# Second layer of a two-layer state-space network: the decay factors move from PSUM to SBUF, and the freed PSUM banks go to other matmul outputs

## What is computed

```
xc = silu(conv2d(x_in));  xz = in_proj(xc);  xm, z = split(xz)
xm = silu(causal_conv1d(xm) + bias)                 # 3 taps, per channel
dt_r, Bm, Cm = split(x_proj(xm));  dt = softplus(dt_proj(dt_r) + dt_b)
for every token t:                                  # 96 channels, 16 states each
    h = exp(dt * A) * h + (dt * xm) * B             # A per channel and state
    y = sum over states of h * C
out = out_proj((y + D * xm) * silu(z)) * silu(x_gate)
```

## Time and profile before

| | |
|---|---|
| median of 3 runs | 1569.81 us (1568.59 to 1570.61) |
| the profiled execution's own time | 1570.93 us |
| its span | 1569.0 us |
| `mid1_phase` in it | from about 676 us to about 1422 us |
| busy shares of the whole span | DVE 77%, PE 74%, ACT 71%, POOL 60% |

### The profile page before, as it was taken

How to read it: one execution, slowest core, us unless ns; L and a number is a source line. 1 busy time by engine, 2 the same in 40 slices (tenths; PEclk the granted TensorE clock), 3 DMA queues, 4 the chain that set the end, 5 groups by cost and what they waited for, 6 DMA issues and landing times. The chain is left out here.

```text
span 1569.0 us, 14783 instructions
## 1 busy us (share of the span) xinstructions
PE 1155.8 (74%) x3828; PEld 423.9 (27%) x3828; DVE 1205.6 (77%) x1198; ACT 1107.2 (71%) x1643; POOL 947.1 (60%) x501
## 2 busy tenths in 40 slices
PE   4899636665643777777888888888888888455995
PEld 2343101111102555422222222222222222002663
DVE  1666539998982777604999999999999999992775
ACT  2687257767642777648889889888888888741664
POOL 2500059999993333216988988888888889850000
PEclk8999855555556999978888888888888888666997
DMA  5455450301002233218878777788777886616572
GB/s 144 123 145 141 98 173 17 108 0 41 14 28 86 84 94 100 76 45 213 191 181 190 183 173 171 178 187 185 177 171 180 183 186 158 155 44 131 127 176 56
DMA packets 137487, 200.56 MB, mean 128 GB/s; under 512 B 27099, under 2 KB 69130, under 8 KB 136916
## 3 DMA queue, kind: packets, MB, share of 16 engines
q1 hardware_dynamic: 133964, 193.27, 50.1%
q0 software_dynamic: 1280, 3.74, 0.8%
q10 hardware_dynamic: 2160, 2.61, 0.7%
HBM read 145.93 MB, written 53.63 MB: 127 GB/s over the span
## 5 line engine op out<-in xcount | busy, mean ns | idle before, releaser
L1802 DVE TENSOR_TENSOR_SCAN m_h<-m_qa,m_state,m_ub 128x512 f32<-128x512 f32 x384 | 464.1, 1263 | 63.7 <-POOL m_ub L1389 56.9
L1389 POOL TENSOR_TENSOR m_ub<-m_dlb,m_bt 128x1536 f32<-128x1536 f32 x128 | 440.4, 3441 | 16.5 <-DMA m_dlb<-scratch_dldu 6.0
L1753 ACT ACTIVATE m_qa<-m_dlb,k_a 128x512 f32<-128x512 f32 x384 | 250.9, 681 | 56.7 <-DVE m_h L1802 52.1
L1813 DVE TENSOR_TENSOR m_g<-m_h,m_qc 128x1536 f32<-128x1536 f32 x128 | 221.4, 1730 | 10.0 <-DVE m_h L1802 8.6
L1596 PE MATMUL m_qm<-m_xa,k_u_taps 96*96 96x512 f32 x192 | 152.3, 959 | 32.3 <-ACT m_sz L1681 31.6
L1635 PE MATMUL m_qy<-m_g,k_seld 128*32 128x512 f32 x768 | 157.9, 697 | 0.0
L1110 POOL TENSOR_TENSOR b_u<-b_dl,b_z 128x1024 f32<-128x1024 f32 x48 | 130.3, 2714 | 17.9 <-ACT b_dl L1000 16.1
L1121 POOL TENSOR_TENSOR b_y<-b_y,b_g 128x1024 f32<-128x1024 f32 x48 | 135.9, 2830 | 3.4 <-DVE b_g L1073 3.2
L1618 PE MATMUL m_qc<-m_cp,k_selc 112*128 112x512 bf16 x128 | 52.3, 409 | 105.7 <-DVE m_g L1813 105.7
L966 PE MATMUL b_qb<-b_bc,k_pack_sel 96*128 96x512 bf16 x96 | 58.9, 613 | 94.8 <-DVE b_u L1051 94.7
L1411 POOL TENSOR_TENSOR m_rest<-m_bcr,m_cp 16x512 f32<-16x512 f32 x32 | 36.9, 1152 | 105.3 <-ACT m_cp L1722 76.1
(11 more groups left out here) (191 smaller groups left out, 2350.5 us busy)
## 6 DMA issues: line engine op xcount, KB each, us to landing
m_dlb<-scratch_dldu SPq DMA_DIRECT2D x128, 384.0 KB, 9.9
m_bt<-scratch_brow SPq DMA_DIRECT2D x128, 256.0 KB, 5.8
scratch_dldu<-m_dldu SPq DMA_DIRECT2D x32, 384.0 KB, 3.2
scratch_z<-a_z SPq DMA_DIRECT2D x24, 256.0 KB
scratch_y<-b_y SPq DMA_DIRECT2D x12, 512.0 KB, 2.6
c_y<-scratch_y SPq DMA_DIRECT2D x16, 384.0 KB, 3.4
scratch_gate<-m_gt SPq DMA_DIRECT2D x32, 192.0 KB, 3.7
scratch_y<-m_yo SPq DMA_DIRECT2D x32, 192.0 KB, 11.5
```

The source lines that it names most:

```text
L1389: nc.gpsimd.tensor_tensor(ub[k % 3][:], dlb[u % 2][:, J:2 * J, :], bcast(bt[u % 2][:, n, :], J), ALU.mult).then_inc(ub_ready, 1)
L1753: nc.scalar.activation(q_a[:, j, :], dlb[u % 2][:, j, :], ACT.Exp, scale=G["a1"][:, j, n:n + 1]).then_inc(da, 1)
L1802: nc.vector.tensor_tensor_scan(h[k % 3][:, j, :], q_a[:, j, :], ub[k % 3][:, j, :], state[:, k % NS, j:j + 1], ALU.mult, ALU.add).then_inc ...
L1813: nc.vector.tensor_tensor(g[k % 2][:], h[k % 3][:], bcast(q_c[:], J), ALU.mult).then_inc(read, 1)
```

## The change

The decay moves to two SBUF buffers, `m_qa0` and `m_qa1`; a decay of step k+1 now waits for the scan of step k-1, not of step k. The three freed banks go out as follows: `m_qm` is split into `m_qu` (causal products) and `m_qz` (z), `m_qg` into `m_qg` (gate) and `m_qt` (dt, B and C rows), and `m_qy` gets a second buffer. With a bank of its own the causal product is no longer evicted to `m_acc`; the SiLU reads `m_qu`. On ACT the softplus of unit t+2 stands in `window` behind the SiLUs, with one table load fewer in each unit, `y_evict` goes to s = 3 and `keep` one step later. On POOL `du_of` goes behind the drive of its step and `outputs` behind `least_of`. On SP the store of y goes to s = 0, ahead of the store of B rows. On PE the projections are dealt out to other steps.

```diff
-        q_a = m.ps("m_qa", [P, J, CH])
-        q_c = m.ps("m_qc", [P, CH])
-        q_y, q_f, q_m = (m.ps(f"m_q{n}", [DI, CH]) for n in ("y", "f", "m"))
-        q_g = m.ps("m_qg", [P, CH])
+        qa = [m.sb(f"m_qa{r}", [P, J, CH]) for r in range(2)]
+        q_y = [m.ps(f"m_qy{r}", [DI, CH]) for r in range(2)]
+        q_f, q_u, q_z, q_g = (m.ps(f"m_q{n}", [DI, CH]) for n in ("f", "u", "z", "g"))
+        q_t, q_c = (m.ps(f"m_q{n}", [P, CH]) for n in ("t", "c"))
...
             def decay(k):
...
-                    if k >= 1:
-                        act.wait_ge(scanned, 3 * (k - 1) + j + 1)
-                    nc.scalar.activation(q_a[:, j, :], dlb[u % 2][:, j, :], ACT.Exp,
+                    if k >= 2:
+                        act.wait_ge(scanned, 3 * (k - 2) + j + 1)
+                    nc.scalar.activation(qa[k % 2][:, j, :], dlb[u % 2][:, j, :], ACT.Exp,
                                          scale=G["a1"][:, j, n:n + 1]).then_inc(da, 1)
...
-                    nc.vector.tensor_tensor_scan(h[k % 3][:, j, :], q_a[:, j, :], ub[k % 3][:, j, :],
+                    nc.vector.tensor_tensor_scan(h[k % 3][:, j, :], qa[k % 2][:, j, :], ub[k % 3][:, j, :],
                                                  state[:, k % NS, j:j + 1], ALU.mult, ALU.add).then_inc(scanned, 1)
...
             def dt_of(v):
...
-                pe.wait_ge(gt_ready, min(v + 2, UNITS))
-                nc.tensor.matmul(q_g[:], G["wdt"][:], xm[v % 4][:], start=True, stop=True).then_inc(dt_mm, 1)
+                if v >= 1:
+                    pe.wait_ge(delta, v)
+                    pe.wait_ge(bc_out, v)
+                    pe.wait_ge(top_out, v)
+                nc.tensor.matmul(q_t[:], G["wdt"][:], xm[v % 4][:], start=True, stop=True).then_inc(dt_mm, 1)
...
-                act.wait_ge(u_mm, v + 1)
-
-                if v >= 1:
-                    act.wait_ge(xm_ready, v)
-                nc.scalar.activation(acc[:], q_m[:], ACT.Identity).then_inc(u_out, 1)
...
             def step(t, s, k):          # GpSimd
+                drive(k + 2)
                 if s == 2:
                     du_of(t + 2)
-                drive(k + 2)
-                if s == 2:
-                    outputs(t - 1)
...
                 if s == 3:
-                    alone(k + 3, t + 3, t)
+                    alone(k + 3, t + 3, t - 1)
                     least_of(t + 2)
+                    outputs(t - 1)
...
             def step(t, s, k):          # ScalarE
                 decay(k + 1)
-                keep(k)
+                keep(k - 1)
+                if s == 0:
+                    rows_out(t + 2)
                 if s == 1:
-                    y_evict(t - 1)
-                    window(t + 4, t + 3)
+                    window(t + 4, t + 3, t + 2)
                 if s == 2:
                     tail_of(t + 5)
-                    u_of(t + 4)
                     middle(t + 2)
                 if s == 3:
-                    softplus(t + 3)
-                if s == 0:
-                    rows_out(t + 2)
+                    y_evict(t - 1)
```

More of the change, by code:

```diff
@@ L1567, in gate_of @@
                     pe.wait_ge(gt_ready, v)
[L1568 to L1572, removed]
+                nc.tensor.matmul(q_g[:], G["gate64"][64:64 + C, :], cva[v % 2][64:64 + C, 0:CH], start=True,
                                  stop=True).then_inc(gate_mm, 1)
@@ L1578, in z_of @@
                 pe.wait_ge(xa_ready, v + 1)
-                pe.wait_ge(u_out, v + 1)
-                nc.tensor.matmul(q_m[:], G["l1_min_z"][:], xa[v % HIST][:, 2:2 + CH], start=True, stop=True).then_inc(z_mm, 1)
+                if v >= 1:
+                    pe.wait_ge(sz_ready, v)
+                nc.tensor.matmul(q_z[:], G["l1_min_z"][:], xa[v % HIST][:, 2:2 + CH], start=True, stop=True).then_inc(z_mm, 1)
             def u_of(v):
@@ L1593, in u_of @@
                 if v >= 1:
-                    pe.wait_ge(sz_ready, v)
+                    pe.wait_ge(xm_ready, v)
                 for k in range(3):
-                    last = nc.tensor.matmul(q_m[:], G["u_taps"][:, k, :], xa[v % HIST][:, k:k + CH], start=(k == 0),
+                    last = nc.tensor.matmul(q_u[:], G["u_taps"][:, k, :], xa[v % HIST][:, k:k + CH], start=(k == 0),
                                             stop=(k == 2))
@@ L1623, in skip_of @@
                 pe.wait_ge(xm_ready, v + 1)
-                nc.tensor.matmul(q_y[:], G["dmat"][:], xm[v % 4][0:DI, :], start=False, stop=False).then_inc(skip_mm, 1)
+                nc.tensor.matmul(q_y[v % 2][:], G["dmat"][:], xm[v % 4][0:DI, :], start=False, stop=False).then_inc(skip_mm, 1)
             def add_up(k):
@@ L1630, in add_up @@
                 pe.wait_ge(read, k + 1)
-                if n == 0 and u >= 1:
-                    pe.wait_ge(y_out, u)
+                if n == 0 and u >= 2:
+                    pe.wait_ge(y_out, u - 1)
                 for j in range(J):
-                    last = nc.tensor.matmul(q_y[32 * j:32 * j + 32, :], G["seld"][:], g[k % 2][:, j, :],
+                    last = nc.tensor.matmul(q_y[u % 2][32 * j:32 * j + 32, :], G["seld"][:], g[k % 2][:, j, :],
                                             start=(n == 0), stop=(n == 3))
@@ L1640, in step @@
                 if s == 0:
+                    skip_of(t - 1)
+                    conv_low(t + 4)
+                if s == 1:
                     z_of(t + 3)
[L1642 to L1644 removed]
                     gate_of(t + 4)
                 if s == 2:
[L1647 removed]
+                    conv_pairs(t + 5)
                     dt_of(t + 3)
                 if s == 3:
[L1650 removed]
+                    u_of(t + 4)
                 c_of(k)
@@ L1657, in _, with window @@
         def _(act):
[L1659 to L1662, removed]
+            def window(a, b, c):
+                if exists(a) or exists(b):
+                    act.preload_act_table_set(SILU_SET)
                 if exists(a):
@@ L1680, in window @@
                         act.wait_ge(y_ready, b - 4)
-                    nc.scalar.activation(sz[b % 5][:], q_m[:], ACT.Silu).then_inc(sz_ready, 1)
-                    act.wait_ge(u_out, b + 1)
+                    nc.scalar.activation(sz[b % 5][:], q_z[:], ACT.Silu).then_inc(sz_ready, 1)
+                    act.wait_ge(u_mm, b + 1)
                     if b >= 4:
@@ L1686, in window @@
                         act.wait_ge(du_ready, b - 3)
-                    nc.scalar.activation(xm[b % 4][0:DI, :], acc[:], ACT.Silu, bias=G["l1_c1b"][:, 0:1]).then_inc(xm_ready, 1)
-                act.preload_act_table_set(LOG_EXP_SET)
+                    nc.scalar.activation(xm[b % 4][0:DI, :], q_u[:], ACT.Silu, bias=G["l1_c1b"][:, 0:1]).then_inc(xm_ready, 1)
+                if exists(a):
+                    act.wait_ge(gate_mm, a + 1)
+                    if a >= 2:
+                        act.wait_ge(gt_stored[a % 2], 16 * (a // 2))
+                    nc.scalar.activation(gt[a % 2][:], q_g[:], ACT.Silu).then_inc(gt_ready, 1)
+                softplus(c)
+                if exists(a) or exists(b) or exists(c):
+                    act.preload_act_table_set(LOG_EXP_SET)
             def tail_of(v):
@@ L1717, in rows_out @@
                     act.wait_ge(brow_stored[v % 4], 16 * (v // 4))
-                nc.scalar.activation(bcr[v % 4][DI:P, :], q_g[DI:P, :], ACT.Identity).then_inc(bc_out, 1)
+                nc.scalar.activation(bcr[v % 4][DI:P, :], q_t[DI:P, :], ACT.Identity).then_inc(bc_out, 1)
                 if v >= 4:
                     act.wait_ge(c_mm, 4 * (v - 4) + 4)
-                nc.scalar.activation(cp[v % 4][DI:DI + NS, :], q_g[DI:DI + NS, :], ACT.Identity).then_inc(top_out, 1)
+                nc.scalar.activation(cp[v % 4][DI:DI + NS, :], q_t[DI:DI + NS, :], ACT.Identity).then_inc(top_out, 1)
             def middle(v):
@@ L1739, in softplus @@
                     act.wait_ge(dldu_stored[v % 2], 16 * (v // 2))
-                nc.scalar.activation(dldu[v % 2][:, 0, :], q_g[0:DI, :], ACT.Softplus).then_inc(delta, 1)
-                act.preload_act_table_set(LOG_EXP_SET)
+                nc.scalar.activation(dldu[v % 2][:, 0, :], q_t[0:DI, :], ACT.Softplus).then_inc(delta, 1)
             def decay(k):
@@ L1762, in y_evict @@
                     act.wait_ge(y_ready, v)
-                nc.scalar.activation(yq[:], q_y[:], ACT.Identity).then_inc(y_out, 1)
+                nc.scalar.activation(yq[:], q_y[v % 2][:], ACT.Identity).then_inc(y_out, 1)
             def keep(k):
```

17 lines of the change are left out of this document (5 added, 12 removed).

## The result

| kernel | median us | ratio to before, 95% interval |
|---|---|---|
| before (same chip) | 1570.21 | |
| changed | 1890.48 (1886.38 to 1893.24) | 1.2031 [1.1995, 1.2067] |

The change costs 320 us; forecast were 1905 us and a range of 1830 to 1995. The profiled execution took 1893.24 us, its span is 1891.4 us.

A forecast was written before the change was run, and what follows sets the result against it. DVE was taken to bound the loop at 5.19 us a step; with scans and POOL's drives excluding each other, 8.04. The loop's +335 us and -1 for the rest on 1570.9 gave 1905 us, range 1830 to 1995.

The forecast's parts named there:

- The bound: Loop of the kernel before: DVE bounds it at 5.19 us a step; at most 24 us of waits can be won.
- The conflict carried over from L1286 to the scan: Scans with two SBUF inputs and POOL's drives exclude each other, as product L1286 and POOL do; chance 0.85.
- The step: Loop: the first scan is blocked until the drive ends; 7.01 us without small products, 8.04 with them, now 5.19.
- The small products: Four POOL products a unit, 1.21 us a step, each slipping between two scans: +1.03 us a step.
- The loop: First scan to last product: 125 steps of 8.04 us, three of 5.19, some 3 us at the end: 1023, +335.
- Start-up: The stretch from 676 to 728 us, before the first scan: a change of 0, +-8 us.
- The PSUM read: Scans lose a PSUM read: 3.5 us less at most, taken as 0; the skill's fixed costs would give 25.
- ACT's Exp into SBUF: On ACT: 681 ns could become 600 or 800, 0.36 us a step, hidden.
- the first rival: Scans take no part in the conflict: DVE stays at 5.19 us a step, 1547 to 1572 us; chance 0.06.
- `window` in one piece: On ACT: four SiLUs, three loads and the softplus, about 6.8 us; fits in 8.04, would overrun at 5.19.
- The third rival: Scans and drives exclude each other and POOL misses DVE's product: 9.7 us a step, 2113 us; chance 0.04.
- the second rival: Scans and drives take turns by element: POOL bounds the loop at 6.2 us a step, 1677 us; chance 0.05.

The follow-up runs named there:

- e6: e2 with `du_of` again ahead of the drive of its step on POOL; result not the reference's: 1543.46 us, ratio 0.9829.
- e1: The kernel before with only the decay moved, to one SBUF buffer in place of the three PSUM banks: 1926.27 us, ratio 1.2257.
- e2: The changed kernel with the scan's second input a PSUM bank of zeros, y eviction at s = 1; result not the reference's: 1602.41 us, ratio 1.0215.
- e3: The changed kernel with each drive made for only the first half of a unit's tokens; result not the reference's: 1692.03 us in one run.
- e4: The changed kernel with each drive replaced by two memsets of zero, which only write SBUF; result not the reference's: 1592.71 us in one run.
- e9: The changed kernel with `du_of` again ahead of the drive of its step on POOL: 1927.88 us, ratio 1.2262.
- e5: The kernel before, decay in PSUM, with `c_of` ahead of `dt_of` on PE at s = 2: 1557.51 us, ratio 0.9922.

## Why the prediction was right

- **The bound.** DVE's stage, 5.19 us a step and 24 us of waits: shown by e6, which runs those 664 us without a gap.
- **The conflict carried over from L1286 to the scan.** The step on which all hung, and no row showed it. e1, e2, e3 and e4 show it: it comes with the second SBUF input alone, goes with it, and follows the length of POOL's reads. Turns by element would have put e3 at 1550 to 1580 us, and it took 1692.
- **The step.** 7.01 us were forecast for a step without small products and 7.01 are measured. That it fits so closely is luck in part: the drive starts 0.14 us after the scans' end and not 0.08, and the hand-over to the scan overlaps by 0.17 and not 0.13.
- **The small products** are the term that was mis-sized, 1.03 us a step: they cost 1.00 (`du_of`), 0.79 (`rest_of`) and 1.76 (both at s = 3), 0.89 in the mean. I had let 0.13 us of each hand-over overlap, by the pairs of the earlier trace rows. Here a small product ends 0.95 us (16 rows) or 1.06 us (96 rows) after the scan that it waits for, 0.20 less than alone, and a scan 1.08 us after the POOL product that it waits for, 0.17 less than alone (medians). With these the term is 1.21 - 0.20 - 0.10 = 0.91.
- **The loop** was put at 1023 us, and ran from 731.8 to the end of its last product, 1741.6: 1009.8. From the first product (751.12) to the 125th (1726.57) a step takes 7.87 us in the mean, 21 us less than forecast in all. Of these, 9 were lost in the first two steps, whose six scans take 19.4 us: the sum had steps of 5.19 us there, but the drives that POOL makes ahead hold off scans as well.

```profile
731.79 19.41 DVE L1791 TENSOR_TENSOR_SCAN m_h<-m_qa,m_state,m_ub 128x512 f32<-128x512 f32 x6 [54.02 <-POOL m_ub L1388]
...
1739.81 1.75 DVE L1802 TENSOR_TENSOR m_g<-m_h,m_qc 128x1536 f32<-128x1536 f32 x1 [0.83 <-issue]
```

- **Start-up:** 0, +-8 was forecast, +3.6 measured (first scan at 731.8 in place of 728.2).
- **The PSUM read:** 0 to 3.5 us were forecast to be won on scans; the shortest scan is 1250 against 1251 ns, so 0. The estimate of 25 us from the Trainium skill, "VectorE: DVE Perf Modes", section "The TRN2 errata — SBUF-src ops pay a fixed extra latency per instruction", is not what this kernel shows.
- **ACT's Exp into SBUF:** 720 in place of 681 ns, inside 600 to 800, and hidden as said.
- **Where it was wrong:** the first rival's time. It put the late `du_of` at 2 us at most over the loop of before; e2 measures 31 us above the kernel before and e6 puts the cost of that one move at 59. The store's and the load's 13 us were set against four steps of 32 us, which was right for the forecast, but not done again for the 20.8 us of the rival. There the 13 are too few: on SP the gate's store and the loads of B come between, so 17.8 us pass in e2, and the drive and `du_of` ahead of them make it 22.5. The fear that `window` in one piece would overrun at 5.19 us a step didn't come true: in e6 no scan waits for a decay.
- **The third rival** didn't come about in the changed kernel, but e1 and e9 are it in part: in each unit POOL once misses DVE's product, and they take 36 and 37 us more than the changed kernel.
- **Two figures of the working** were read wrong, and nothing hangs on them. ACT's work was set against 5.27 us a step, but 454 DVE instructions in 610 us, four a step, make it 5.37. And the second rival's 0.53 us for a scan isn't the most that L1282 allows: 954 ns for 768 columns allow 0.64, which would make that rival's time 1724 us in place of 1677.

## What to carry to other kernels

Before a buffer is moved from PSUM to SBUF, count the SBUF inputs of every DVE instruction that reads it, and look at what GpSimd reads beside it: the second SBUF input can turn two engines that overlap into two that take turns. Here the price was the whole time of GpSimd's products less what falls beside DVE's other product, and a step went from 5.19 to 7.9 us. An instruction that is blocked in this way shows as busy and long, not as waiting, so compare its shortest instance with its median. And an order that is free at one pitch isn't at another: the same move of one product won 59 us at steps of 5.2 us (e6) and lost 37 at 7.9 (e9).

## What the runs showed that was not expected

- A POOL product over 16 rows holds off a scan over 128 rows as well: `m_rest`, 16x512, adds 0.79 us to a step. The sum had taken that for granted, and no row showed it.
- A small POOL product that has waited behind a scan needs 0.20 us less than alone, not only the 0.13 us of the earlier trace rows.
- e5 took 12 us off the kernel before, where the waits that it was aimed at came to 8.6. A wait costs more than its idle time: in the kernel before, a step with 0.96 us of this wait takes 6.27 us (scans at 1000.27 and 1006.54) in place of 5.19, and nine of those make 9.7. The rest stays open.
